# One sum moved from GpSimd to VectorE, and half of a convolution moved earlier on TensorE, in the mixer of a decoder layer

## The chip, the cores and the metric

The kernel runs on one core of one Trainium2 chip. The metric is the device time of one launch in microseconds. The kernel before took 1225.16 us, the median of three runs (1222.33, 1225.16 and 1227.24 us).

## What is computed

One decoder layer on 16 sequences of 256 tokens with 512 features, in three steps, each added to its input:

```python
x = x + attention(layernorm(x))
x = x + xattn(ctx, ctx, layernorm(x), ssm_kernel, D, 8)   # a long convolution per head
x = x + ffn(layernorm(x))                                 # values rounded to 127 levels

# xattn, per head h of 8 features: kv[i,j,l] = k[i,l] * v[j,l]
#   y = causal convolution of kv with ssm_kernel[h], plus D[h] * kv
#   out[j,l] = sum_i y[i,j,l] * q[i,l]
# ffn: gate, up = split(q(x) @ q(w_gate_up).T)
#      q(silu(gate) * up) @ q(w_down).T, q = round to a row's largest value / 127
```

The change lies in the second and third step, which one part of the kernel (`mixer`) computes together.

## The kernel before

The program has two blocks. The first (`attention`) fills the span up to about 634 us and is not touched by the change. The second (`mixer`) works head by head: 32 heads (`NH = 32`), each of which covers 8 rows of `x` for all 16 sequences, that is 128 rows of 512 features. It is written as a software pipeline of 33 rounds, `r = 0` to `32`, all unrolled. Each engine has a `body(r, p)` with a fixed order of work, and semaphores tie the engines together. Round `r` holds the convolution of head `r`, the mixed values and the second residual of head `r - 1`, the first half of the FFN (gate, up, silu, hidden values) of head `r - 2`, and the second half of the FFN (down projection, scale, output sum) of head `r - 3`. Rounds 0 and 1 also prepare the FFN's weights.

What one full round does on each engine, in the order of its queue, with the names used below and their lines:

- TensorE (PE): `conv(r, p, lt)` for `lt` = 0 to 3 are the four block rows of the convolution, of 6, 12, 18 and 24 matmuls of 288 columns (L1197 to L1199). Each one is two halves of equal size, and `halves=(0,)` or `(1,)` takes one of them. They write `y_ps[lt % 2]`, so that convolution 2 needs the products of convolution 0 to be done, and convolution 3 those of convolution 1. The order is: convolution 0, the first FFN matmul group (`gate_up`, L1255), convolution 1, `hidden_turned` (11 transposes of the FFN's rounded hidden values, L1234), `mixed` (4 transposes of `yT`, L1218), FFN matmuls and the down projection (L1267), convolution 2, `queries` (L1209), half of convolution 3, `tokens_turned` (L1242), the other half of convolution 3. `mixed` of head `r - 1` waits until GpSimd has written all four parts of `yT` of that head.
- VectorE (DVE): `products(r, p, lt)` multiplies each convolution block by the query (four instructions, L1630 to L1642) and signals GpSimd. Among them stand the statistics of two layer norms (L1604, L1612), the scaling of gate and up (L1706, L1712), the second residual (L1666), `down_scaled` (L1689), the largest hidden values (`hidden_max`, L1647) and `hidden_scale`, four instructions on one column (L1653 to L1659). The end of a round on this queue is `products 2`, `hidden_max 2`, `hidden_scale`, `products 3`.
- GpSimd (POOL): `first_norm` of head `r + 1` (L1529, L1531, L1570), `tree(0)`, `hiddens 0` (L1560), the norm of head `r - 1`, `hiddens 1`, `tree(1)`, `hiddens 2`, `outs` (L1552), `tree(2)`, `tree(3)`. A `tree` sums a product tile in three instructions (L1538, L1540, L1545), the last of which writes a part of `yT`. `outs` adds `down` and `x2_held`, both in SBUF, to `y_out`.
- ScalarE (ACT): silu, the rounding of tokens and hidden values, and copies out of PSUM. `hold` copies the second residual to `x2_held`.
- SyncE (SP): loads and stores. The store of `y_out` waits for `out_done`, and the loads of the next convolution stand behind it in the queue.

After round 32 a tail finishes the last two heads. `outs(NH - 2)` is in it.

Of the kernel before, what the change touches and what calls it, by code (L numbers as in the profile page):

```python
# [20 lines left out]
ALU = mybir.AluOpType  # L21
# [14 lines left out]
NH, HJ = 32, 8  # L36
# [16 lines left out]
def reached(eng, sem, value):  # L53

    if not isinstance(value, int) or value > 0:
        eng.wait_ge(sem, value)
# [949 lines left out]
def mixer(nc, ctx, x1d, x_stored, sd, w2, W, out, eye_f, eye_b, half_neg2, eps2, toep_0, kv_0, toep_loaded, kv_loaded, load_conv_of):  # L1006
# [30 lines left out]
    yt_full, x2_done, hold_done = sem("yt_full"), sem("x2_done"), sem("hold_done")  # L1037
# [67 lines left out]
    x2_held = sb("x2_held", [P, D], F32)  # L1105
# [48 lines left out]
    with nc.Block() as block:  # L1154
# [29 lines left out]
        def _(pe):  # L1184
# [104 lines left out]
            def weights(r, k):  # L1289

                if not isinstance(r, int) or r > 1:
                    return
                for n, o in enumerate(SETS):
                    if o[0] == 5 * r + k:
                        turn_set(n)
# [11 lines left out]
            def body(r, p, loop=False):  # L1307
                conv_live, ffn_live, down_live = live(r, loop), live(r - 2, loop), live(r - 3, loop)
                if isinstance(r, int) and r == 2:
                    for side in range(2):  # L1310
                        pe.wait_ge(taken[side], sum(o[3] == side for o in SETS))
                if isinstance(r, int) and r == 1:
                    banks_taken(6)
                if isinstance(r, int) and r == 0:
                    banks_taken(4, 5)
                if conv_live:
                    conv(r, p, 0)
                weights(r, 1)
                if ffn_live:
                    gate_up(r - 2, 0, (0,))  # L1320
                if isinstance(r, int) and r == 0:
                    banks_taken(2, 3)
                if conv_live:
                    conv(r, p, 1)
                weights(r, 2)
                if down_live:
                    hidden_turned(r - 3, 0)
                    hidden_turned(r - 3, 1)
                if live(r - 1, loop):
                    mixed(r - 1, 1 - p)  # L1330
                if ffn_live:
                    gate_up(r - 2, 0, (1,))
                    gate_up(r - 2, 1, (0,))
                if down_live:
                    project_down(r - 3, 0)
                if ffn_live:
                    gate_up(r - 2, 1, (1,))
                if down_live:
                    project_down(r - 3, 1)
                if ffn_live:  # L1340
                    gate_up(r - 2, 2)
                if conv_live:
                    conv(r, p, 2)
                weights(r, 3)
                if live(r + 1, loop):
                    queries(r + 1)
                if conv_live:
                    conv(r, p, 3, (0,))
                weights(r, 4)
                if live(r - 1, loop):  # L1350
                    tokens_turned(r - 1)
                if conv_live:
                    conv(r, p, 3, (1,))
                weights(r, 5)
# [170 lines left out]
        @block.gpsimd  # L1525
        def _(pool):
            def inv_std(done, h, mv, var, var_done, rstd, rstd_done):
                pool.wait_ge(done, h + 1)
                nc.gpsimd.tensor_tensor(var[:], mv[:, 1:2], eps2[:], ALU.add).then_inc(var_done, 1)  # L1529
                pool.wait_ge(var_done, h + 1)  # L1530
                nc.gpsimd.tensor_tensor(rstd[:], var[:], half_neg2[:], ALU.pow).then_inc(rstd_done, 1)  # L1531

            def tree(h, p, lt):

                n, w = h * LT + lt + 1, HJ * HB
                pool.wait_ge(prod_done, n)
                pr = prod[lt % 2]
                nc.gpsimd.tensor_tensor(tree4[:], pr[:, :, 0:4 * w], pr[:, :, 4 * w:8 * w], ALU.add).then_inc(t4_done, 1)  # L1538
                pool.wait_ge(t4_done, n)
                nc.gpsimd.tensor_tensor(tree2[:], tree4[:, :, 0:2 * w], tree4[:, :, 2 * w:4 * w], ALU.add).then_inc(t2_done, 1)  # L1540
                pool.wait_ge(t2_done, n)

                if lt == 0:
                    reached(pool, yt_full, h - 1)
                nc.gpsimd.tensor_tensor(yT[p][:, lt, :].rearrange("p (a c) -> p a c", a=2), tree2[:, :, 0:w],  # L1545
                                        tree2[:, :, w:2 * w], ALU.add).then_inc(yT_done, 1)

            def outs(h):
                pool.wait_ge(down_done, h + 1)
                pool.wait_ge(hold_done, h + 1)  # L1550
                reached(pool, out_stored, h * 32)
                nc.gpsimd.tensor_tensor(y_out[:], down[:], x2_held[:], ALU.add).then_inc(out_done, 1)  # L1552

            def hiddens(h, c):
                at, w = CH[c]
                pool.wait_ge(silu_done, h * 3 + c + 1)
                pool.wait_ge(up_done, h * 3 + c + 1)

                reached(pool, ht_done, h * 3 + c - 2)
                nc.gpsimd.tensor_tensor(hid[:, at:at + w], silu[:, at:at + w], up[:, at:at + w], ALU.mult).then_inc(hid_done, 1)  # L1560

            def first_norm(h):

                inv_std(mv2_done, h, mv2, var2, var2_done, rstd2, rstd2_done)
                count = h + 1
                if not isinstance(h, int):
                    pool.lower_val(count)
                alone(pool, rstd2_done)
                pool.wait_ge(rstd2_done, count)
                nc.gpsimd.tensor_scalar(shift2[:], mv2[:, 0:1], rstd2[:, 0:1], -1.0, ALU.mult, ALU.mult).then_inc(shift2_done, 1)  # L1570

            first_norm(0)

            def body(r, p, loop=False):
                conv_live, ffn_live = live(r, loop), live(r - 2, loop)
                if live(r + 1, loop):
                    first_norm(r + 1)
                if conv_live:
                    tree(r, p, 0)
                if ffn_live:  # L1580
                    hiddens(r - 2, 0)
                if live(r - 1, loop):
                    inv_std(mv3_done, r - 1, mv3, var3, var3_done, rstd3, rstd3_done)
                if ffn_live:
                    hiddens(r - 2, 1)
                if conv_live:
                    tree(r, p, 1)
                if ffn_live:
                    hiddens(r - 2, 2)
                if live(r - 3, loop):  # L1590
                    outs(r - 3)
                if conv_live:
                    tree(r, p, 2)
                    tree(r, p, 3)

            rounds(pool, body)
            for c in range(len(CH)):
                hiddens(NH - 1, c)
            outs(NH - 2)

        @block.vector
        def _(dve):
# [47 lines left out]
            def hidden_scale(h, p):  # L1650

                dve.wait_ge(hmax3_done, 3 * (h + 1))
                nc.vector.tensor_reduce(hmax[:], hmax3[:], AX_X, ALU.max).then_inc(hmax_done, 1)  # L1653
                dve.wait_ge(hmax_done, h + 1)
                nc.vector.tensor_scalar(sh[p][:], hmax[:], sx[p][:, 0:1], QMAX * EPS_Q, ALU.mult, ALU.max).then_inc(sh_done, 1)
                dve.wait_ge(sh_done, h + 1)
                nc.vector.reciprocal(sh_rec[:], sh[p][:]).then_inc(shr_done, 1)
                dve.wait_ge(shr_done, h + 1)
                nc.vector.tensor_scalar(sh_inv[:], sx[p][:], sh_rec[:, 0:1], QMAX, ALU.mult, ALU.mult).then_inc(shi_done, 1)  # L1659
# [25 lines left out]
            def down_scaled(h, p, to):  # L1685
                dve.wait_ge(d_full, h + 1)

                reached(dve, out_done, min(h, NH - 1) if isinstance(h, int) else h)
                nc.vector.scalar_tensor_tensor(out=to[:], in0=a_ps[:], scalar=sh[p][:, 0:1], in1=s2_b[:],  # L1689
                                               op0=ALU.mult, op1=ALU.mult).then_inc(down_done, 1)  # L1690

            def last_out():
                dve.wait_ge(down_done, NH)
# [62 lines left out]
            def body(r, p, loop=False):  # L1756
# [49 lines left out]
                if ffn_live:  # L1806
                    hidden_max(r - 2, 2)
                    hidden_scale(r - 2, p)
                if conv_live:
                    products(r, p, 3)  # L1810
                weights(r, 5)
# [9 lines left out]
            for c in range(len(CH)):  # L1821
                whole(NH - 1, c)
            down_scaled(NH - 2, 0, down)
            down_scaled(NH - 1, 1, last_down)
            last_out()

# [34 lines left out]
```

## Time and profile before

| | us |
|---|---|
| median of three runs | 1225.16 |
| the profiled execution | 1222.95 |
| its span in the profile | 1221.1 |

| engine | busy, share of the span |
|---|---|
| PE (matmul) | 93% |
| DVE | 82% |
| POOL | 77% |
| ACT | 72% |

The 1.85 us between the span and the time of that execution lie outside what the profile covers. Shares over the whole span mix the attention block with the mixer; from about 700 us on, the round repeats itself and can be read from two neighbouring rounds. A timeline row gives the start, the duration, engine, line, operation, output and inputs; a bracket at its end gives how long the engine sat idle before it and which instruction ended that. Two instructions of one engine can overlap a little in the records, because the next one starts while the last results of the one before are still being written; what counts in a sum is the distance from start to start. The granted TensorE clock is 1.00 of full speed (2.4 GHz) in all of this stage.

### The profile page before, as it was taken

Reading aid. Unit: us, or ns where it says so; the run is one execution under the profiler, and the core shown is the slowest. Engines: PE = TensorE matmul, PEld = TensorE weight load, DVE = VectorE, ACT = ScalarE, POOL = GpSimd, SP = SyncE. Lnnn points to the kernel's source line nnn. Section 1 sums busy time; section 2 is a strip of 40 time slices with the busy share of each in tenths; the row PEclk is TensorE's granted clock in tenths of the full one; section 3 lists DMA queues with packets and bytes.
Section 4 is the critical chain, followed back from the end, with each engine's and each line's share of the span. In section 5 each row is a group of like instructions: output and inputs, shape, how many; then the busy total and the mean of one; then the engine's idle time right before and its main releaser. Section 6 shows DMA issues by size and latency. Waiting matters only on the chain. (4 is left out here: it accounts for less than half of the span.)

```text
span 1221.1 us, 31917 instructions
## 1 busy us (share of the span) xinstructions
PE 1130.7 (93%) x10114; PEld 814.0 (67%) x10114; DVE 1002.1 (82%) x3147; ACT 878.4 (72%) x1811; POOL 945.4 (77%) x1085
## 2 busy tenths in 40 slices
PE   7889999999999999998768899999999999999996
PEld 6777777878777787776446566666666666666662
DVE  5678888878787887887768788988889888898875
ACT  3878878878787887887746566667666676666764
POOL 0377787767778776877736799999999999999983
PEclk9989999999999999999679999999999999999999
DMA  6345655556555555566675433444434443344410
GB/s 213 101 165 183 187 169 159 186 168 194 181 167 169 166 174 185 180 207 191 235 230 190 146 105 129 137 147 137 115 127 137 148 137 114 129 137 148 134 32 26
DMA packets 88342, 188.84 MB, mean 155 GB/s; under 512 B 12351, under 2 KB 29017, under 8 KB 88089
## 3 DMA queue, kind: packets, MB, share of 16 engines
q1 hardware_dynamic: 87353, 186.74, 48.7%
q10 hardware_dynamic: 864, 0.66, 0.3%
q8 instruction: 51, 0.84, 0.3%
q14 instruction: 74, 0.61, 0.2%
HBM read 107.57 MB, written 54.62 MB: 133 GB/s over the span
## 5 line engine op out<-in xcount | busy, mean ns | idle before, releaser
L780 ACT ACTIVATE prob<-masked,negmax 128x128 f32<-128x128 f32 (+1 forms) x512 | 206.4, 454 | 73.6 <-DVE negmax L915 72.6
L915 DVE CUSTOM_DVE_ANT_0 masked<-s_ps,mask_f 128x128 f32<-128x128 f32 (+1 forms) x512 | 161.1, 352 | 29.7 <-PE s_ps L661 14.9
L1255 PE MATMUL f_ps<-wqkv,xiT 128*128 128x512 bf16 (+1 forms) x768 | 174.5, 364 | 2.4 <-DVE up L1712 1.5
L1538 POOL TENSOR_TENSOR tree<-prod 128x512 f32<-128x512 f32 x128 | 163.1, 1274 | 10.6 <-DVE prod L1642 10.4
L1446 ACT ACTIVATE silu<-gate,sx 128x512 f32<-128x512 f32 (+1 forms) x96 | 66.0, 687 | 136.1 <-DVE gate L1706 136.1
L539 POOL TENSOR_TENSOR kv_s<-kv_f,kv_s 128x1152 f16<-128x1152 f32 x64 | 152.3, 2379 | 4.6 <-ACT kv_s L794 4.6
L921 DVE TENSOR_TENSOR pT_lo<-t_ps,pT_hi 128x384 f16<-128x384 f32 x256 | 140.6, 550 | 15.4 <-ACT pT_hi L788 15.1
L532 POOL TENSOR_TENSOR kv_f<-c_in 128x1024 f32<-128x1024 f32 x64 | 146.0, 2281 | 0.2 <-DMA c_in<-in_ctxr 0.2
L788 ACT CAST pT_hi<-t_ps 128x384 f16<-128x384 f32 x256 | 122.2, 478 | 29.7 <-PE t_ps L670 28.5
L598 PE MATMUL g_ps<-x_all,wqkv 128*128 128x256 f16 x512 | 140.1, 274 | 3.1 <-DVE x_all L879 3.1
L599 PE MATMUL g_ps<-x_all,wqkv 128*128 128x256 f16 x512 | 140.1, 274 | 0.0
L600 PE MATMUL g_ps<-x_all,wqkv 128*128 128x256 f16 x512 | 140.0, 273 | 0.0
L670 PE MATMUL t_ps<-eye_f,prob 128*128 128x128 f32 x768 | 130.3, 279 | 0.0
L1255 PEld LDWEIGHTS f_ps<-wqkv,xiT 128*128 128x128 bf16 x768 | 75.1, 98 | 72.2 <-DVE up L1712 2.7
L1560 POOL TENSOR_TENSOR hid<-silu,up 128x512 f32<-128x512 f32 (+1 forms) x96 | 113.5, 1183 | 10.4 <-DVE up L1712 5.6
L1630 DVE TENSOR_TENSOR prod<-y_ps,qT 128x512 f32<-128x512 f32 x128 | 87.0, 680 | 36.0 <-PE y_ps L1199 34.5
L523 POOL TENSOR_TENSOR att<-att,bv_b 128x128 f32<-128x128 f32 x128 | 55.7, 457 | 75.5 <-DVE att L932 75.5
L685 PE MATMUL o_ps<-v_hi,pT_hi 128*128 128x33 f16 x768 | 85.7, 180 | 29.9 <-DVE pT_lo L921 22.9
L685 PEld LDWEIGHTS o_ps<-v_hi,pT_hi 128*128 128x128 f16 x768 | 67.9, 97 | 56.8 <-DVE pT_lo L921 35.6
L1540 POOL TENSOR_TENSOR tree<-tree 128x256 f32<-128x256 f32 x128 | 93.5, 731 | 10.0
L670 PEld LDWEIGHTS t_ps<-eye_f,prob 128*128 128x128 f32 x768 | 94.6, 144 | 0.1
L1197 PE MATMUL y_ps<-kv,x_all 128*128 128x288 f16 x320 | 92.2, 288 | 1.5 <-DVE x_all L1724 1.5
(187 smaller groups left out, 3591.9 us busy)
## 6 DMA issues: line engine op xcount, KB each, us to landing
kv_pairs<-kv_s SPq DMA_DIRECT2D x64, 576.0 KB, 3.4
kv<-kv_pairs SPq DMA_DIRECT2D x32, 1152.0 KB, 8.6
c_in<-in_ctxr SPq DMA_DIRECT2D x64, 192.0 KB, 2.5
q_st<-w_raw SPq DMA_DIRECT2D x192, 64.0 KB, 2.0
k_st<-w_raw SPq DMA_DIRECT2D x192, 64.0 KB, 2.0
x_all<-in_x SPq DMA_DIRECT2D x16, 512.0 KB, 6.6
x_res<-in_x SPq DMA_DIRECT2D x16, 512.0 KB, 6.1
x_after_attention<-x_out SPq DMA_DIRECT2D x16, 512.0 KB, 4.4
```

What stands on the lines that cost most here:

```text
L532: nc.gpsimd.tensor_tensor(f[:, :, 0:4 * w].rearrange("p m (d c) -> p m d c", d=4), c[:, :, None, 0:w].broadcast_to([P, PM, 4, w]), shifted ...
L539: nc.gpsimd.tensor_tensor(kv_s[k % 2][:, 1], kv_f[k % 2][:], kv_s[k % 2][:, 0], ALU.subtract).then_inc(kv_low, 1)
L598: nc.tensor.matmul(dst, ah, bh, start=t == 0, stop=False)
L599: nc.tensor.matmul(dst, ah, bl, start=False, stop=False)
L600: mm = nc.tensor.matmul(dst, al, bh, start=False, stop=t == DT - 1)
L670: mm = nc.tensor.transpose(t_ps[h % 2][:, c * P:(c + 1) * P], prob[h % 2][:, c * P:(c + 1) * P], eye_f[:])
L685: nc.tensor.matmul(dst, ph, v_hi[p][:, kt, head, 0:VW], start=kt == 0, stop=False)
L780: ins = nc.scalar.activation(prob[h % 2][:, at:at + w], masked[h % 2][:, at:at + w], ACT.Exp, bias=negmax[:, h % 2, t:t + 1], scale=-1.0)
L915: ins = nc.vector.tensor_tensor_reduce(masked[h % 2][:, at:at + w], s_ps[h % 2][:, at:at + w], mask_f[:, S - w:S], -1.0, FAR, ALU.add, ALU ...
L921: nc.vector.tensor_tensor(pT_lo[h % 2][:], t_ps[h % 2][:, 0:PCOL], pT_hi[h % 2][:], ALU.subtract).then_inc(plo_done, 1)
L1255: mm = nc.tensor.matmul(f_ps[side][:, 0:w], xiT[:, t, :], w1T[:, t, side * I_FF + at:side * I_FF + at + w], start=t == 0, stop=t == DT - 1)
L1538: nc.gpsimd.tensor_tensor(tree4[:], pr[:, :, 0:4 * w], pr[:, :, 4 * w:8 * w], ALU.add).then_inc(t4_done, 1)
```

## The change

Two edits. The output sum of head `r - 3` moves from GpSimd (between `hiddens 2` and `tree(2)`) to VectorE, between `hidden_scale` and `products 3`; likewise in the tail, right behind `down_scaled(NH - 2)`. And the first half of convolution 2 moves on TensorE from behind the FFN matmuls to in front of `hidden_turned`.

```diff
@@ tensor: body @@
                 weights(r, 2)
+                if conv_live:
+                    conv(r, p, 2, (0,))
                 if down_live:
                     hidden_turned(r - 3, 0)
                     hidden_turned(r - 3, 1)
...
                 if conv_live:
-                    conv(r, p, 2)
+                    conv(r, p, 2, (1,))
                 weights(r, 3)
@@ gpsimd @@
-            def outs(h):
-                pool.wait_ge(down_done, h + 1)
-                pool.wait_ge(hold_done, h + 1)
-                reached(pool, out_stored, h * 32)
-                nc.gpsimd.tensor_tensor(y_out[:], down[:], x2_held[:], ALU.add).then_inc(out_done, 1)
...
-                if live(r - 3, loop):
-                    outs(r - 3)
                 if conv_live:
                     tree(r, p, 2)
                     tree(r, p, 3)
...
-            outs(NH - 2)
@@ vector @@
+            def outs(h):
+                for count in (h + 1, h * 32):
+                    if not isinstance(count, int):
+                        dve.lower_val(count)
+                dve.wait_ge(hold_done, h + 1)
+                dve.wait_ge(down_done, h + 1)
+                reached(dve, out_stored, h * 32)
+                nc.vector.tensor_tensor(y_out[:], down[:], x2_held[:], ALU.add).then_inc(out_done, 1)
...
                     hidden_scale(r - 2, p)
+                if live(r - 3, loop):
+                    outs(r - 3)
                 if conv_live:
                     products(r, p, 3)
...
             down_scaled(NH - 2, 0, down)
+            outs(NH - 2)
             down_scaled(NH - 1, 1, last_down)
```

Since all rounds are unrolled, `h` is a plain number everywhere and `lower_val` adds nothing.

## Rows read from the trace of the kernel before

**Rows 1.** Busy time by windows: stretch, width, then busy time per engine, PE clock, DMA.

```profile
900.00:1000.00 100.00, 97.22 (x695) 64.38 (x693) 88.75 (x237) 67.06 (x123) 94.34 (x125) 1.00 0.42 133
```

**Rows 2.** Timeline of POOL, one round: start, duration, engine, line, operation.

```profile
1002.62 0.19 POOL L1529 TENSOR_TENSOR var<-mv,eps 128x1 f32<-128x1 f32 x1
...
1006.41 1.27 POOL L1560 TENSOR_TENSOR hid<-silu,up 128x512 f32<-128x512 f32 x1
...
1012.24 1.00 POOL L1560 TENSOR_TENSOR hid<-silu,up 128x384 f32<-128x384 f32 x1
1013.20 1.27 POOL L1552 TENSOR_TENSOR y_out<-down,x_held 128x512 f32<-128x512 f32 x1
1014.42 1.27 POOL L1538 TENSOR_TENSOR tree<-prod 128x512 f32<-128x512 f32 x1
...
1016.99 1.28 POOL L1538 TENSOR_TENSOR tree<-prod 128x512 f32<-128x512 f32 x1
...
1019.57 0.19 POOL L1529 TENSOR_TENSOR var<-mv,eps 128x1 f32<-128x1 f32 x1
```

**Rows 3.** Timeline of PE over the same round.

```profile
1002.71 0.66 PE L1218 MATMUL a_ps<-eye_f,yT 128*128 128x128 f32 x4 [0.45 <-POOL yT L1545]
...
1013.80 0.29 PE L1197 MATMUL y_ps<-kv,toep 128*128 128x288 f16 x1
...
1015.27 0.29 PE L1197 MATMUL y_ps<-kv,x_all 128*128 128x288 f16 x1
...
1018.43 0.33 PE L1234 MATMUL f_ps<-eye_b,hid_i 128*128 128x128 bf16 x3
...
1019.66 0.33 PE L1218 MATMUL a_ps<-eye_f,yT 128*128 128x128 f32 x1 [0.46 <-POOL yT L1545]
```

**Rows 4.** Timeline of DVE over the same round.

```profile
1004.37 0.68 DVE L1712 TENSOR_TENSOR up<-f_ps,s_b 128x512 f32<-128x512 f32 x1
...
1013.27 0.55 DVE L1647 TENSOR_REDUCE hmax<-hid 128x1 f32<-128x384 f32 x1
...
1014.49 0.21 DVE L1659 TENSOR_SCALAR sh_inv<-sx,sh_rec 128x1 f32<-128x1 f32 x1
1015.47 0.69 DVE L1630 TENSOR_TENSOR prod<-y_ps,qT 128x512 f32<-128x512 f32 x1 [0.77 <-PE y_ps L1199]
...
1016.68 0.21 DVE L1642 TENSOR_TENSOR prod<-y_ps,qT 128x64 f32<-128x64 f32 x1
...
1019.32 0.17 DVE L1612 BATCH_NORM_AGGREGATE mv<-st 128x2 f32<-128x6 f32 x1
```

**Rows 5.** Timeline of DVE and POOL at the end of round 2.

```profile
693.12 0.22 DVE L1659 TENSOR_SCALAR sh_inv<-sx,sh_rec 128x1 f32<-128x1 f32 x1
693.25 0.68 DVE L1630 TENSOR_TENSOR prod<-y_ps,qT 128x512 f32<-128x512 f32 x1
...
693.17 0.73 POOL L1540 TENSOR_TENSOR tree<-tree 128x256 f32<-128x256 f32 x1
```

**Rows 6.** Timeline of POOL: `tree(3)` of rounds 2 and 31, 29 rounds apart.

```profile
694.74 1.27 POOL L1538 TENSOR_TENSOR tree<-prod 128x512 f32<-128x512 f32 x1 [0.32 <-DVE prod L1642]
...
1186.38 1.27 POOL L1538 TENSOR_TENSOR tree<-prod 128x512 f32<-128x512 f32 x1 [0.46 <-DVE prod L1642]
```

**Rows 7.** Timeline of DVE and POOL at 10 and 61 us, and line L532.

```profile
10.31 2.29 DVE L940 SCALAR_TENSOR_TENSOR wqkv<-w_raw,wqkv 128x2048 f16<-128x2048 f32 x1 [1.31 <-ACT wqkv L800]
...
61.45 2.40 DVE L940 SCALAR_TENSOR_TENSOR wo_lo<-w_raw,wo_hi 128x2048 f16<-128x2048 f32 x1
...
60.82 0.88 POOL L523 TENSOR_TENSOR att<-att,bv_b 128x128 f32<-128x128 f32 x2
61.65 4.31 POOL L532 TENSOR_TENSOR kv_f<-c_in 128x1024 f32<-128x1024 f32 x1
...
L532 POOL TENSOR_TENSOR kv_f<-c_in x64: 2228/2248/4308, 36.8 to 608.4; 128x1024 f32<-128x1024 f32 x64
```

**Rows 8.** Groups by line and shape: the sum of two SBUF tiles on DVE.

```profile
L1694 DVE TENSOR_TENSOR x_q<-x_t,x 128x512 f32<-128x512 f32 x1 | 0.7, 691 | 0.0
```

## The prediction

> **What bounds the kernel now.** I read the page first for the stage: the change touches only the mixer, and there the table by windows says that in 100 us PE is busy 97 us, POOL 94 us, DVE 89 us, at the full clock [rows 1]. That doesn't say which one sets the time, so I went to the timeline of one round, engine by engine. The first rows of two neighbouring rounds on POOL give the period: 1019.57 - 1002.62 = 16.95 us [rows 2]. Over 29 rounds it is the same: (1186.38 - 694.74) / 29 = 16.95 us [rows 6]. Everything that the change does has to show in this number, times 29.
>
> Then I looked for what closes a loop of 16.95 us, because in a pipeline the longest loop is the bound. There are two, of nearly the same length.
>
> Loop 1 is POOL's own queue. It has no gap other than a fixed 0.17 us inside the norm: the output sum starts at 1013.20, `tree(2)` at 1014.42, `tree(3)` at 1016.99, the next norm at 1019.57 [rows 2]. The sum costs 1014.42 - 1013.20 = 1.22 us of it.
>
> Loop 2 runs through PE. `mixed` waits 0.45 us for the last `yT` [rows 3]; from its start at 1002.71 PE works without a stop until the end of convolution 3, at 1015.27. Then come DVE's `products 3` (it waited 0.77 us for PE, starts 1015.47, its last instruction ends 1016.68 + 0.21 = 1016.89 [rows 4]), POOL's `tree(3)` (1016.99 to 1019.57 [rows 2]) and `mixed` again at 1019.66 [rows 3]. That is 16.95 us too. So taking 1.22 us off POOL alone would gain nothing, as `tree(3)` would only wait for the products; and moving matmuls alone would gain nothing, as POOL stays full.
>
> **The change, part by part.**
>
> *Half of convolution 2 moved.* Twelve such matmuls take 1015.27 - 1013.80 = 1.47 us [rows 3], so the moved nine take 1.10 us. Between the end of convolution 3 and `mixed` PE has work until about 0.45 us before `mixed` may start; with 1.10 us more there the stall goes and `mixed` starts up to 1.10 - 0.45 = 0.65 us later, measured from the end of convolution 3, than the data would allow. Loop 2 is cut: what is left of it is PE's own work, at most 16.95 - 0.45 = 16.50 us a round. The 11 transposes in front of `mixed` move back by 1.10 us, which only gives ScalarE more time. What hangs behind `mixed` (second residual, up, gate) comes up to 0.65 us later. Its cover: up 0 is done at 1004.37 + 0.68 = 1005.05 and POOL takes it at 1006.41 [rows 2, 4], so 1.36 us are free. I cost this edit at nothing, and if the cover failed it would be some tenths of a us per round.
>
> *The sum off POOL.* Minus 1.22 us in front of `tree(2)`, whose products are ready by then (DVE is past them when it does `hidden_max 2`). `tree(2)` ends earlier, and `tree(3)` then waits for `products 3`, since these stand behind `hidden_scale`.
>
> *The sum on DVE.* It stands in a place that was free only as long as PE was late: DVE sat 0.77 us before `products 3` [rows 4]. With loop 2 cut, a third loop comes up, through both engines. From POOL's norm to the end of `hiddens 2`: 1002.62 to 1012.24, and `hidden_max 2` starts 1013.27, so 10.65 us [rows 2, 4]. From there to the end of `hidden_scale`: 1014.49 - 1013.27 = 1.22, and 0.13 until the next instruction can start, the distance that round 2 shows (693.25 - 693.12) [rows 4, 5]: 1.35 us. Then the sum, P. Then `products 3`, `products 0`, statistics, gate 0 and the aggregate: 1015.47 to 1019.32, 3.85 us, and 0.17 + 0.08 us until POOL's norm starts at 1019.57 [rows 2, 4]. Together 10.65 + 1.35 + 3.85 + 0.25 = 16.10 us plus P. The queue decides P. The three waits in front of the sum are long met: `down_scaled` stands much earlier in the same round of DVE's queue, and `hold` and the store of the last `y_out` belong to the round before.
>
> What is queued behind it: `products 3`, for which `tree(3)`, and then `mixed`, wait. The store of `y_out` starts about 1.3 us later than before, and the loads of the next convolution with it on SP's queue; they have a whole round before they are needed, so nothing.
>
> *P, its lower bound.* The only sum of two SBUF tiles of this size on DVE takes 0.69 us [rows 8], like the other 512-column instructions, which follow each other at 0.60 us. P = 0.60 gives 16.70 us.
>
> *P, its upper bound.* In the whole steady stage no DVE instruction reads two tiles from SBUF; each has one in PSUM or has one input only. The trace has one place where such an instruction meets a working POOL, at 61 us. There POOL's addition took 4.31 us where its median over 64 is 2.25 us, and it ended (65.96) 2.11 us after DVE's (63.85) [rows 7]: it stood still for as long as DVE ran. And DVE's own took 2.40 us where the same shape took 2.29 us beside an idle POOL. It had started at 61.45 with a POOL instruction running until 60.82 + 0.88 = 61.70, so it seems to have waited 0.11 us, until 0.14 us before that one's recorded end. So the two keep each other out, and who comes second waits for the whole of the other's reading.
>
> Who comes second here? Round 2 has no output sum yet, so its POOL queue already has the new order. There the second instruction of `tree(2)` starts at 693.17 and the place of the new sum on DVE opens at 693.25 [rows 5]. DVE is 0.08 us late, and it would wait until 0.14 us before 693.17 + 0.73 = 693.90, that is until 693.76: 0.51 us. P = 0.60 + 0.51 = 1.11 us and the period is 16.10 + 1.11 = 17.21 us. At worst it waits for the full 693.90 and a little more, P = 1.3 us and 17.4 us.
>
> The phase is fixed by the loop itself: `hiddens 2` releases both `tree(2)` on POOL and `hidden_max 2` on DVE, so the 0.08 us repeat in every round. I take 1.11 us, because the row nearest to this case (two SBUF inputs beside a working POOL) shows the wait and its size. A POOL instruction may read nothing in its first hundredths of a us, which shrinks the 0.08 us to perhaps 0.03 or 0.04; that is the weak step.
>
> The Trainium skill has this as a rule, on its page "SBUF — State Buffer", section "Who interferes with whom": a VectorE instruction with two SBUF inputs shares a read port with GpSimd, the port is held for a whole instruction, and whoever comes second blocks. The trace agrees at 61 us (4.31 against 2.25 us) [rows 7]. The same section says that a VectorE instruction with one SBUF input doesn't contend, which would make the sum's old place free of it and the new one not.
>
> **The sum.** Each of 29 rounds goes from 16.95 to 17.21 us: 29 x 0.26 = 7.5 us. Rounds 0 and 1 have no output sum, and the moved matmuls fill no stall that matters there. In the tail DVE waits for PE's last matmuls when the last moved sum comes, so nothing. The profiled execution would go from 1222.95 to 1230.5 us. That execution lay 2.2 us under the median of the three; against the median, 1225.16, the forecast is 1232.7 us.
>
> **The rivals.**
>
> *DVE comes first.* If the sum gets in before the second instruction of `tree(2)`, DVE waits for nothing, P is 0.60 and POOL waits instead. It can: it would finish `tree(2)` by about 0.3 us before `products 3` are ready. The period is 16.70 us, 29 x 0.25 = 7.2 us are gained: 1218.0 us against the median. For it: the margin is 0.08 us or less. Against: DVE's start is the later one in round 2, and it has three waits in front of it instead of two. The point from which it decides is a start on DVE some 0.05 us earlier. This is the rival on the other side.
>
> *In between.* The wait is shorter than a whole instruction, or some rounds go one way and some the other; or PE's loop stays for a reason that I don't see (ScalarE's hidden values late for `hidden_turned`) and holds 16.95 us while DVE's wait stays hidden. P from 0.75 to 0.95 us gives 16.85 to 17.05 us, 1222.3 to 1228.1 us, 1225 us in the middle. A change that doesn't do what it says, with PE still waiting for `yT`, ends here too.
>
> **How the numbers follow.** Forecast 0.58, DVE first 0.25, in between 0.17. About 0.5% (6.1 us) is what a measurement of this kernel can tell from no change; counted from 1225.2 that is 1219.0 and 1231.3. The forecast's own range is 1229.5 to 1237 (an error of 0.05 us in the period is 1.5 us, and the runs before differ by 5 us), of which some seven tenths lie above 1231.3; the gain of the first rival, 7.2 us, lies just over the line, two thirds of its chance count as faster. Slower: 0.45, with the upper edge of the third case; same: 0.36; faster: 0.19. The range goes from 1217.5 to 1237 us, as it has to take in most of the first rival.
>
> **What would show it.** The period of the rounds: 17.21, 16.70 or between. The new sum on DVE: about 1.2 us long in the records if it waits, 0.69 if not. If it waits, `tree(2)`'s second instruction stays at 0.73 us; if DVE is first, that one grows to some 1.3 us. `mixed` no longer waits for `yT` directly behind the transposes, POOL idles about 1 us before `tree(3)` with `products 3` as the releaser. Wrong would be: a PE stall that stays at 0.45 us, or DVE starved in the up and gate steps behind a later `mixed`.

## The result

The changed kernel takes 1229.94 us (median of 20 runs, 1224.32 to 1235.4) and the kernel before, over as many runs, 1222.43 us. The ratio is 1.0046, with a 95% interval of 1.0031 to 1.0060, which is 5.6 us slower (3.8 to 7.3). This ratio is an estimate over the runs and not the quotient of the two medians, which lie 7.5 us apart; the two means lie 6.2 us apart. Runs of one kernel differ by 10 or 11 us, so the times alone give the difference only to within some 2 us. The profiled execution has a span of 1230.9 us.

The round of the mixer in the changed kernel, first on POOL, then on DVE, then on PE (timelines, columns as in [rows 2]):

```profile
1002.67 0.79 POOL L1547 TENSOR_TENSOR yT<-tree 128x128 f32<-128x128 f32 x1
1004.54 1.27 POOL L1540 TENSOR_TENSOR tree<-prod 128x512 f32<-128x512 f32 x1 [1.09 <-DVE prod L1635]
...
1016.77 1.00 POOL L1556 TENSOR_TENSOR hid<-silu,up 128x384 f32<-128x384 f32 x1
1017.73 1.27 POOL L1540 TENSOR_TENSOR tree<-prod 128x512 f32<-128x512 f32 x1
1019.08 0.73 POOL L1542 TENSOR_TENSOR tree<-tree 128x256 f32<-128x256 f32 x1
1019.88 0.79 POOL L1547 TENSOR_TENSOR yT<-tree 128x128 f32<-128x128 f32 x1
1021.76 1.28 POOL L1540 TENSOR_TENSOR tree<-prod 128x512 f32<-128x512 f32 x1 [1.09 <-DVE prod L1635]
...
1017.80 0.55 DVE L1640 TENSOR_REDUCE hmax<-hid 128x1 f32<-128x384 f32 x1 [0.34 <-POOL hid L1556]
...
1019.03 0.21 DVE L1652 TENSOR_SCALAR sh_inv<-sx,sh_rec 128x1 f32<-128x1 f32 x1
1019.16 1.19 DVE L1692 TENSOR_TENSOR y_out<-down,x_held 128x512 f32<-128x512 f32 x1
1020.27 0.68 DVE L1623 TENSOR_TENSOR prod<-y_ps,qT 128x512 f32<-128x512 f32 x1
...
1004.52 0.30 PE L1197 MATMUL y_ps<-kv,toep 128*128 128x288 f16 x1 [0.85 <-DVE prod L1635]
...
1007.72 0.61 PE L1218 MATMUL a_ps<-eye_f,yT 128*128 128x128 f32 x4
```

The period, `tree(3)` to `tree(3)`, is 1021.76 - 1004.54 = 17.22 us where it was 16.95 us [rows 2, 6]. What to see, line by line: POOL has lost its full queue and waits 1.09 us for `products 3`. `mixed` on PE no longer waits for `yT` (0.45 us in [rows 3]); PE's wait has moved to convolution 1, which waits 0.85 us for `products 3`. And DVE's sum, free to start at 1019.16, is recorded with 1.19 us; alone it takes 0.69 us [rows 8]. At 1019.08, 0.08 us earlier, POOL had begun the second instruction of `tree(2)`, which kept its 0.73 us; the third, which came while the sum was running, took 0.79 us where it takes 0.46 us otherwise. The instruction behind the sum starts 1.11 us after it.

The waiting counts as work. In the table by windows (columns as in [rows 1]) DVE's busy time rose from 89 to 94 us in 100. Of what the sum adds there, about 4 us are the sum itself (0.68 us in each of 5.8 rounds) and about 3 us are waiting (0.51 us in each); the longer rounds take back a little more than 1 us:

```profile
900.00:1000.00 100.00, 94.39 (x672) 63.20 (x682) 94.17 (x239) 65.63 (x122) 87.87 (x118) 1.00 0.44 135
```

The same sum over all rounds, by the view of one tile (count, then shortest/median/longest duration in ns, then the first and the last start in us):

```profile
L1692 DVE TENSOR_TENSOR y_out<-down,x_held x31: 680/1189/1199, 709.5 to 1222.5; 128x512 f32<-128x512 f32 x31
```

`tree(3)` of round 2 starts at 694.85 us (before 694.74) and that of round 31 at 1193.21 (before 1186.38): 29 rounds cost 498.36 us instead of 491.64, that is 6.7 us more. Of the difference between the two profiled spans, 1230.9 - 1221.1 = 9.8 us, nearly all of the rest is 3.0 us in the tail behind the last round (37.7 against 34.7 us). There the granted TensorE clock was 0.75 in the changed kernel's first 7 us, against 1.00 before; this is taken up at the end.

### The profile page after: what moved, and what is told of

Same layout as the page of the kernel before. It is cut to its first block and busy times, and to the rows that moved or that the text cites. A ratio compares the mean times of both kernels' runs of the same rounds, so it can differ in the third digit from the quotient of the medians.

```text
span 1230.9 us, 31855 instructions
## 1 busy us (share of the span) xinstructions
PE 1127.8 (92%) x10052; PEld 813.9 (66%) x10114; DVE 1033.2 (84%) x3178; ACT 875.2 (71%) x1811; POOL 918.7 (75%) x1054
## 5 line engine op out<-in xcount | busy, mean ns | idle before, releaser
L1255 PE MATMUL f_ps<-wqkv,xiT 128*128 128x512 bf16 (+1 forms) x736 | 169.8, 367 | 4.8 <-ACT xiT L1441 1.1
L532 POOL TENSOR_TENSOR kv_f<-c_in 128x1024 f32<-128x1024 f32 x64 | 146.1, 2283 | 0.7 <-DMA c_in<-in_ctxr 0.7
L1197 PE MATMUL y_ps<-kv,toep 128*128 128x288 f16 x320 | 91.7, 287 | 13.5 <-DVE prod L1635 12.7
```

The costliest lines, as they stand in the source:

```text
L532: nc.gpsimd.tensor_tensor(f[:, :, 0:4 * w].rearrange("p m (d c) -> p m d c", d=4), c[:, :, None, 0:w].broadcast_to([P, PM, 4, w]), shifted ...
L1197: nc.tensor.matmul(dst, toep[p][:, 0, taps], c[:, 0, m], start=mt == 0, stop=False)
L1255: mm = nc.tensor.matmul(f_ps[side][:, 0:w], xiT[:, t, :], w1T[:, t, side * I_FF + at:side * I_FF + at + w], start=t == 0, stop=t == DT - 1)
```

## Experiments

The theory is that of the forecast. The sum reads two SBUF tiles; while POOL reads, it can't, and the other way round; whoever comes second waits for the other's instruction. The sum stands in a loop through both engines (the third loop of the forecast), of 16.10 us without it. The rivals are that the moved half convolution costs the time, that the sum costs 1.2 us at any place and in any order, and that any instruction there would cost what the sum costs. The period stands for each kernel as the mean of the 29 distances between `tree(3)` of round 2 and of round 31; before it is 16.95 us, in the changed kernel 17.19 us (17.19 to 17.22 us in the middle rounds; the last one, in which POOL and DVE have no next head to prepare, is 16.23 us, before 16.50 us).

### One half of the change each

```diff
 # e1_sum_only: the changed kernel, but
-                if conv_live:
-                    conv(r, p, 2, (0,))
...
-                    conv(r, p, 2, (1,))
+                    conv(r, p, 2)
```

> The changed kernel with convolution 2 whole again at its old place; only the sum is on VectorE. Theory (the sum waits for GpSimd and lengthens the loop norm - hiddens 2 - hidden_scale - sum - products 3): the loop doesn't contain the moved matmuls, so the period stays at 17.2 us, the sum takes 1.2 us in the records, and the time is that of the changed kernel, some 0.5% over the kernel before. Rival (the moved half convolution delays mixed and with it up and gate, and that costs the time): the period goes back to 16.95 us and the ratio to 1.000.

Measured: ratio 0.9989 (0.9971 to 1.0008), period 16.93 us. The sum is recorded with 0.68 us (median), not 1.2. So my expectation was wrong, and the rival's numbers (16.95 us and 1.000) were nearly right. Taken by itself, this run would say that the moved matmuls cost the time.

```diff
 # e2_conv_only: the kernel before, but
+                if conv_live:
+                    conv(r, p, 2, (0,))
...
-                    conv(r, p, 2)
+                    conv(r, p, 2, (1,))
```

> The kernel before with only the half of convolution 2 moved; the sum stays on GpSimd. Theory: GpSimd's queue is full for 16.95 us, so the period stays 16.95 us and the ratio is 1.000 within 0.002; TensorE's 0.45 us wait for yT goes and comes back as a wait for the products of convolution 3 or 1. Rival (the moved matmuls cost the time): a period over 17.1 us and a ratio of 1.004 or more.

Measured: ratio 1.0001 (0.9970 to 1.0032), period 16.95 us, as expected. One detail was not: `mixed` still waits 0.22 us for `yT`, where I expected that wait to go. The moved matmuls cost nothing and bring nothing by themselves. Neither half makes the kernel slower; both together do.

The trace of the first kernel says how. POOL and DVE at the end of its round:

```profile
1016.16 1.00 POOL L1554 TENSOR_TENSOR hid<-silu,up 128x384 f32<-128x384 f32 x1
1017.27 1.27 POOL L1538 TENSOR_TENSOR tree<-prod 128x512 f32<-128x512 f32 x1
1018.62 1.20 POOL L1540 TENSOR_TENSOR tree<-tree 128x256 f32<-128x256 f32 x1
...
1016.98 0.21 DVE L1633 TENSOR_TENSOR prod<-y_ps,qT 128x64 f32<-128x64 f32 x1
...
1018.55 0.68 DVE L1690 TENSOR_TENSOR y_out<-down,x_held 128x512 f32<-128x512 f32 x1
1019.37 0.69 DVE L1621 TENSOR_TENSOR prod<-y_ps,qT 128x512 f32<-128x512 f32 x1
```

With convolution 2 whole at its late place, `products 2` end at 1016.98 + 0.21 = 1017.19, so `tree(2)` starts at 1017.27, which is 1.11 us after the start of `hiddens 2` and not 0.96 us as in the changed kernel (1016.77 to 1017.73). These 0.15 us carry the second instruction of `tree(2)` from 0.08 us ahead of the sum to 0.07 us behind it (1018.62 against 1018.55). Now DVE is first, the sum takes 0.68 us and it is POOL's instruction that is recorded with 1.20 us, in time that POOL has to spare. What holds this kernel at 16.93 us is PE's loop through `mixed` (loop 2 of the forecast), which the moved half convolution had cut: `mixed` waits 0.43 or 0.44 us for `yT` here, as in the kernel before. So the moved matmuls take part, but through a race: by freeing `products 2` from PE they let POOL start 0.15 us sooner.

The same profile holds the opposite case. In round 30 `products 2` come early, DVE waits 0.32 us for `hiddens 2`, and `tree(2)` starts 0.96 us after the start of `hiddens 2`, as in the changed kernel:

```profile
1171.12 0.73 POOL L1540 TENSOR_TENSOR tree<-tree 128x256 f32<-128x256 f32 x1
1171.19 1.20 DVE L1690 TENSOR_TENSOR y_out<-down,x_held 128x512 f32<-128x512 f32 x1
```

POOL is 0.07 us ahead, the sum takes 1.20 us, and this round takes 17.53 us where the ones before it take 16.92 or 16.93 us. In the 27 rounds before it DVE was ahead, by 0.04 to 0.08 us, and the sum took 0.68 us each time. The kernel and its instructions are the same in both cases; what differs is when `products 2` are done, and with that the order.

### The same place with one input

```diff
 # e3_one_input: the changed kernel, but
-                nc.vector.tensor_tensor(y_out[:], down[:], x2_held[:], ALU.add).then_inc(out_done, 1)
+                nc.vector.tensor_reduce(y_out[:, 0:1], down[:], AX_X, ALU.max).then_inc(out_done, 1)
```

> The changed kernel with the sum replaced, in the same place and with the same waits and signal, by the maximum of one tile (down, 512 columns, one SBUF input, 0.68 us alone); the output sum is left out, so the output isn't the layer's. Theory (two SBUF inputs make VectorE wait for GpSimd): no wait, the instruction takes 0.68 us, the period is 16.10 + 0.60 = 16.70 us, 29 x 0.25 = 7.2 us under the kernel before, ratio 0.994. Rival (any instruction at this place costs what the sum costs, by its waits or its place): 1.2 us in the records and 17.2 us.

Measured: ratio 0.9924 (0.9901 to 0.9948), period 16.70 us, the instruction 0.675 us. The place and the three waits cost nothing; an instruction of the same length that reads one tile adds 0.60 us to the loop, and the sum 1.11 us. The bound of 16.70 us that the forecast gave for P = 0.60 is met.

The replacement also writes one column only, where the sum writes 512. That the writing isn't the cause can be seen in the changed kernel, in two instructions of `products` that read one tile in PSUM and one in SBUF and write 384 columns to SBUF:

```profile
1003.66 0.54 DVE L1629 TENSOR_TENSOR prod<-y_ps,qT 128x384 f32<-128x384 f32 x1
...
1004.98 0.54 DVE L1629 TENSOR_TENSOR prod<-y_ps,qT 128x384 f32<-128x384 f32 x1
```

During the first one POOL was idle; the second one started in the middle of the first instruction of `tree(3)` (1004.54 to 1005.81), which reads and writes SBUF. Both took 0.54 us, and POOL's took its 1.27 us.

### One wait more on GpSimd

```diff
 # e4_pool_yields: the changed kernel, but in tree(h, p, lt)
+                if lt == 2:
+                    reached(pool, out_done, min(h - 2, NH - 3))
                 pool.wait_ge(t4_done, n)
                 nc.gpsimd.tensor_tensor(tree2[:], tree4[:, :, 0:2 * w], tree4[:, :, 2 * w:4 * w], ALU.add)...
```

> The changed kernel with one wait more, on GpSimd: the second instruction of tree(2) waits until the sum on VectorE is done. The sum itself and its place are as in the changed kernel. Theory (the one who comes second waits, and GpSimd has about 1.1 us to spare there): the sum takes 0.69 us, GpSimd's second instruction starts some 0.8 us later and tree(2) still ends just before products 3, period 16.70 to 16.75 us, ratio 0.994 to 0.995. Rival (an added wait on a full engine can only cost; the length of the sum has another cause): the sum stays at 1.2 us and the period at 17.2 us or more.

Measured: ratio 0.9918 (0.9891 to 0.9945), period 16.70 us, and the sum 0.68 us. The sum over all rounds by the view of one tile, and `tree(2)` and the start of `tree(3)` on POOL's timeline:

```profile
L1694 DVE TENSOR_TENSOR y_out<-down,x_held x31: 679/681/693, 712.7 to 1208.7; 128x512 f32<-128x512 f32 x31
...
1012.09 1.27 POOL L1540 TENSOR_TENSOR tree<-prod 128x512 f32<-128x512 f32 x1
1014.29 0.73 POOL L1544 TENSOR_TENSOR tree<-tree 128x256 f32<-128x256 f32 x1 [0.93 <-DVE y_out L1694]
1015.10 0.46 POOL L1549 TENSOR_TENSOR yT<-tree 128x128 f32<-128x128 f32 x1
1015.62 1.28 POOL L1540 TENSOR_TENSOR tree<-prod 128x512 f32<-128x512 f32 x1
```

The same two-input sum at the same place on DVE; only POOL now gives way. POOL waits 0.93 us for it, and `tree(3)` follows with no wait for `products 3` left, so POOL's time to spare is just used up. A wait added to one engine makes the kernel 1.3% faster than the changed one (0.9918 / 1.0046 = 0.987; the 29 rounds account for 498.36 - 484.34 = 14.0 us of it, 1.1%).

### The sum earlier in the queue

```diff
 # e6_earlier: the changed kernel, but hidden_scale(h, p, between=None) has, behind its second instruction
+                if between:
+                    between()        # outs(r - 3)
```

> The changed kernel with the sum two short instructions earlier, between the second and the third instruction of hidden_scale, 0.45 us before its place in the changed kernel. There the first instruction of tree(2) is still running, for another 0.29 us, and the second hasn't started. Theory: the sum waits 0.15 us, is recorded with 0.8 to 0.9 us, and now the second instruction of tree(2) waits for it (recorded with over 1.0 us instead of 0.73); the loop gets 0.63 us instead of 1.13 from it, period 16.7 us, ratio 0.992 to 0.995. Rival (the sum's 1.2 us are its own length beside a working GpSimd, whatever comes first): 1.2 us again and a period of 17.2 us.

Measured: ratio 0.9933 (0.9907 to 0.9960), period 16.73 us.

```profile
1008.67 0.21 DVE L1648 TENSOR_SCALAR sh<-hmax,sx 128x1 f32<-128x1 f32 x1
1008.80 0.83 DVE L1694 TENSOR_TENSOR y_out<-down,x_held 128x512 f32<-128x512 f32 x1
1009.55 0.15 DVE L1652 RECIPROCAL sh_rec<-sh 128x1 f32<-128x1 f32 x1
...
1007.81 1.27 POOL L1540 TENSOR_TENSOR tree<-prod 128x512 f32<-128x512 f32 x1
1009.16 1.05 POOL L1542 TENSOR_TENSOR tree<-tree 128x256 f32<-128x256 f32 x1
```

Starting 0.44 us sooner behind `hiddens 2` than in the changed kernel, the sum meets the end of the instruction before: it waits 0.83 - 0.68 = 0.15 us, until about 1008.95, where POOL's first instruction has its recorded end at 1009.08. Then it is POOL's second one that waits (1.05 instead of 0.73 us). Both engines are seen waiting in turn, each by the other's rest.

```diff
 # e5_before_max: the changed kernel, but
+                if live(r - 3, loop):
+                    outs(r - 3)
                 if ffn_live:
                     hidden_max(r - 2, 2)
                     hidden_scale(r - 2, p)
-                if live(r - 3, loop):
-                    outs(r - 3)
```

> The changed kernel with the sum on VectorE between products 2 and hidden_max 2, that is about 1.6 us earlier in the queue, where VectorE sat 0.34 us waiting for hiddens 2. Theory (who comes second waits until 0.14 us before the other's recorded end): the sum starts while hiddens 2 runs on GpSimd, waits some 0.2 us for it, and hidden_max 2 starts about 0.43 us after hiddens 2 instead of directly behind it; tree(2)'s first instruction then waits for the sum, in time that GpSimd has to spare. The sum adds 0.43 us to the loop instead of 1.13: period 16.10 + 0.43 = 16.53 us, some 12 us under the kernel before, ratio 0.990. Rival (the sum costs its length wherever it stands, and a blocked GpSimd costs too): a period of 16.9 us or more.

Measured: 1212.21 us against 1225.93 us, ratio 0.9877 (0.9848 to 0.9906), period 16.53 us. This version beats both kernels, with the same instructions as the changed one.

```profile
1007.81 0.93 DVE L1692 TENSOR_TENSOR y_out<-down,x_held 128x512 f32<-128x512 f32 x1
1008.66 0.54 DVE L1640 TENSOR_REDUCE hmax<-hid 128x1 f32<-128x384 f32 x1
...
1007.18 1.00 POOL L1556 TENSOR_TENSOR hid<-silu,up 128x384 f32<-128x384 f32 x1
1008.15 1.71 POOL L1540 TENSOR_TENSOR tree<-prod 128x512 f32<-128x512 f32 x1
```

The sum starts in the 0.34 us in which DVE waited for `hiddens 2` anyway, and waits 0.25 us for it: until about 1008.06, 0.12 us before `hiddens 2`'s recorded end at 1008.18. `hidden_max 2` starts 1008.66 - 1008.18 = 0.48 us behind that end instead of 0.03 us: the sum costs the loop 0.45 us. `tree(2)` waits 0.44 us (1.71 instead of 1.27), in spare time.

### Useless work in two places

Both kernels have one instruction more per round, the maximum of 256 columns into a scratch column; the two places are some 3 us apart.

```diff
 # e7_filler: in front of products 2;  e8_filler_late: in front of outs
+                    nc.vector.tensor_reduce(filler[:], down[:, 0:256], AX_X, ALU.max)
```

> The changed kernel with one useless instruction more per round on VectorE: the maximum of 256 columns of down into a scratch column, in front of products 2, 0.33 us from start to start. Theory (a race of 0.07 us between the sum and the second instruction of tree(2) decides): products 2 end 0.33 us later, still before hidden_max 2 is released, but tree(2) now starts for the products and not directly behind hiddens 2, some 0.15 us later. Its second instruction then comes behind the sum, the sum takes 0.68 us, and the period falls to 16.7 us, ratio 0.992 to 0.995, though more work was added. Rival (the useless instruction adds to a busy engine): the period stays at 17.2 us or grows to 17.5 us.

Measured: ratio 0.9921 (0.9894 to 0.9948), period 16.73 us.

```profile
1011.64 1.27 POOL L1541 TENSOR_TENSOR tree<-prod 128x512 f32<-128x512 f32 x1
1013.00 1.22 POOL L1543 TENSOR_TENSOR tree<-tree 128x256 f32<-128x256 f32 x1
...
1012.94 0.68 DVE L1693 TENSOR_TENSOR y_out<-down,x_held 128x512 f32<-128x512 f32 x1
```

The sum now starts 0.06 us ahead of POOL's second instruction instead of 0.08 us behind it (0.04 to 0.07 us in all rounds but the last, where it is 0.16 us). This is the race of the first experiment, brought about without touching PE: 0.32 us of useless work on DVE a round takes 0.46 us off the round. It shows by what the moved matmuls took part, namely when `products 2` are done.

> The same useless instruction, this time directly in front of the sum, on the chain that sets the period. Theory: in the changed kernel the sum only waits there for the second instruction of tree(2), which is read until 0.5 us after the sum could start; 0.33 us of other work go into that wait. The sum is recorded with about 0.86 us instead of 1.20, and the period stays at 17.2 us, the ratio at that of the changed kernel. Rival (the sum is slow by itself beside a working GpSimd): the sum stays at 1.2 us and the period grows by 0.33 us to 17.55 us, 9.6 us in all.

Measured: ratio 1.0054 (1.0033 to 1.0075), period 17.24 us, and the sum with 0.87 us.

```profile
1016.92 0.41 DVE L1813 TENSOR_REDUCE filler<-down 128x1 f32<-128x256 f32 x1
1017.25 0.87 DVE L1693 TENSOR_TENSOR y_out<-down,x_held 128x512 f32<-128x512 f32 x1
1018.04 0.68 DVE L1624 TENSOR_TENSOR prod<-y_ps,qT 128x512 f32<-128x512 f32 x1
```

The distance from the useless instruction to `products 3` is 1018.04 - 1016.92 = 1.12 us, as from the sum alone in the changed kernel (1.11 us). So 0.33 us of work in the chain that sets the period add only some 0.03 us to a middle round (17.22 to 17.25 us instead of 17.19 to 17.22): the sum had been waiting for that long. A sum that is slow by itself would have stayed at 1.2 us.

## Why the prediction was right, and where its sizes were off

- **The bound.** Two loops of 16.95 us, POOL's queue and PE through `mixed`. Each half of the change alone leaves the period at 16.93 and 16.95 us. Shown. The stall of `mixed` didn't go by the moved matmuls alone (0.22 us are left), only in the changed kernel.
- **The moved half convolution at nothing.** Shown for the kernel before (1.0001). Its cover for up 0 held: in the changed kernel up 0 ends at 1009.91 and POOL's `hiddens 0` takes it at 1010.93, without a wait. But the step missed something: it costed the edit by itself, and not what an earlier `products 2` does to the phase of `tree(2)`. The forecast said that `hiddens 2` releases both `tree(2)` and `hidden_max 2`, so that the loop itself fixes the phase. That holds only where `products 2` are done before `hiddens 2`. It took the phase from round 2, where they are (DVE waits 0.86 us for `hiddens 2` there), and the moved matmuls happen to bring that about in 28 of the 29 rounds; this was not worked out, and that the phase was right is in part luck. For the sum alone it would have been wrong, as my expectation for that experiment was.
- **The third loop, 16.10 us plus P.** 16.70 us with the one-input instruction (P = 0.60), 17.22 us with the sum (P = 1.11; from 1004.54 to 1021.76): both within 0.01 us of the forecast.
- **P = 1.11 us, not 0.60.** The forecast had one support for it, the meeting of two instructions at 61 us [rows 7], and it held. The release point taken from there (0.14 us before the recorded end) came back as about 0.13 and 0.12 us in the two kernels with the sum earlier. The Trainium skill's rule on the page "SBUF — State Buffer", section "Who interferes with whom", is that the pair of ports that the two engines share is an exclusive lock and that the order of issue decides who blocks. All the runs here agree: 1.19 us for the sum behind POOL, 0.68 us ahead of it, with the one that waits let in about 0.13 us before the other's recorded end.
- **Who is second.** 0.08 us were forecast, and it was 0.07 to 0.10 us in 28 of the 29 rounds. The rival "DVE comes first" was the true alternative: with a wait on POOL or with useless work DVE is first, at 16.70 and 16.73 us, and 16.70 us was its forecast.
- **The time.** The forecast was 7.5 us more. Measured were 5.6 us by the ratio (3.8 to 7.3), so 7.5 us lies just outside its interval; that the two medians are also 7.5 us apart proves nothing. The term that was too large is 29 x 0.26: the rounds aren't all alike, the last one takes 16.23 us against 16.50 us before, and together they give 6.7 us. The 1232.7 us were counted from a median of three runs that lay 2.7 us above that of twenty. The step from 6.7 to 5.6 us stays in the noise. (Round 2 has no output sum either, not only rounds 0 and 1; the 29 rounds counted are 3 to 31, so the count is right.) With the step that decided it resting on some hundredths of a microsecond, the wide range and the chances near one half were what the profile allowed.
- **What DVE's sum would look like**, 1.2 us long, POOL idle about 1 us before `tree(3)`, no wait of `mixed`: as forecast.

## What to carry to other kernels

Before an elementwise operation is moved from GpSimd to VectorE, count its SBUF inputs: with two of them it waited here for a GpSimd instruction that was reading SBUF, and its cost is up to its own length plus the rest of GpSimd's instruction. Then its place in the queue decides; here 0.04 us ahead and 0.07 us behind gave opposite results: put it where VectorE waits anyway and GpSimd has time to spare behind it, or make GpSimd wait for it. And when two halves of a change are each neutral but cost time together, look for two instructions that have changed places in time.

## What was not expected

The waiting is inside the recorded duration of the waiting instruction, on both engines (1.19 against 0.68 us, 1.71 against 1.27 us), so the view of waits and the idle columns show nothing of it, and the engine looks busier. It is found by the spread of one line's durations: 680 to 1199 ns for one shape.

The changed kernel has a free instance of the race in its last full round, where `tree(2)` waited 0.27 us for `products 2`, so that DVE came first:

```profile
1191.13 0.68 DVE L1692 TENSOR_TENSOR y_out<-down,x_held 128x512 f32<-128x512 f32 x1
1191.29 1.11 POOL L1542 TENSOR_TENSOR tree<-tree 128x256 f32<-128x256 f32 x1
```

The tail behind the last round varied from 33.2 to 37.7 us between the profiled executions. In the windows of the tail the granted clock of the changed kernel is 0.75 and in the kernel before 1.00:

```profile
1193.20:1200.00 6.80, 4.91 (x25) 2.42 (x26) 2.71 (x5) 3.85 (x7) 3.53 (x4) 0.75 0.12 37
...
1186.40:1193.00 6.60, 4.74 (x32) 2.68 (x33) 3.19 (x7) 4.41 (x8) 3.93 (x6) 1.00 0.00 0
```

The order of the tail is the same in both kernels but for the last sum. Over all ten profiles the length of the tail goes with this clock. Cut into stretches of 7 us from the start of the last `tree(3)`, the first four have a granted clock of 1.00 in the tail of 33.2 us (the sum only). In the five tails of 34.7 and 34.8 us, the kernel before among them, one of them is at 0.76 or 0.77. In the tail of 36.2 us two are at 0.76, and in the three of 37.5 to 37.7 us two are at 0.76 or less, one of these at 0.54 to 0.63.

Whether the changed kernel's tail is slower in every execution can't be seen, as each kernel has one profile. But the longest tails are not bound to the time of the rounds: the two kernels with useless work have them at periods of 16.73 and 17.24 us. The mean granted clock, which every run has, speaks for a matter of the single execution too. At a mean clock of 0.972 the changed kernel took 1232.6 us (3 runs) and the kernel before, in the runs beside the first four experiments, 1226.4 us (8 runs); at 0.976 they took 1228.8 us (4 runs) and 1222.6 us (5 runs). At the same clock that is 6.2 us both times, close to the 6.7 us of the rounds, and the profiled executions had 0.972 (changed) and 0.976 (before). So a part of their 9.8 us is likely the clock; this is argued from few runs, taken at different times.
